# A layer of attention and feed-forward: the vector engine's turn in another order, the sums beside their compares, the window mask in the maximum

## Time and profile before

| | us |
|---|---|
| median of 3 runs (lowest, highest) | 1960.08 (1959.28, 1961.83) |
| the profiled execution | 1959.31 |
| its span, first to last instruction | 1957.5 |
| busy: PE, DVE, ACT, POOL | 1876.3, 1433.4, 1229.4, 1235.9 |
| stretch of the turns | about 22 to 1540 |
| a group of four turns in the loop | 46.8 |

### The profile page before, as it was taken

One profiled execution on the slowest core, in us unless ns is written; L12 is line 12 of the kernel. 1 busy time (PEld: TensorE's weight loads), 2 busy tenths in 40 slices (PEclk: granted clock), 3 DMA queues, 4 the chain that ended last, 5 costly groups with the idle time before them and its releaser, 6 DMA issues.

```text
span 1957.5 us, 42161 instructions
## 1 busy us (share of the span) xinstructions
PE 1876.3 (96%) x11698; PEld 1252.8 (64%) x11698; DVE 1433.4 (73%) x3926; ACT 1229.4 (63%) x4840; POOL 1235.9 (63%) x1150
## 2 busy tenths in 40 slices
PE   4999999999999999999999999999989979999997
PEld 3667677777777777776777676777666635444443
DVE  6998888888888888888888888888899644302022
ACT  5777777777777777777777777776666535312121
POOL 3777777777777777777777777777677521212121
PEclk8999999999999999999999999999999989999999
DMA  5000000000000000000000000000100042000000
GB/s 199 25 26 25 26 25 24 24 24 24 32 25 24 24 24 24 29 24 24 24 24 24 30 29 24 24 24 13 54 13 7 7 134 79 26 1 22 0 21 21
DMA packets 44353, 61.43 MB, mean 31 GB/s; under 512 B 4928, under 2 KB 18496, under 8 KB 44288
## 3 DMA queue, kind: packets, MB, share of 16 engines
q1 hardware_dynamic: 44288, 60.64, 9.6%
HBM read 47.97 MB, written 12.65 MB: 31 GB/s over the span
## 4 chain that ended last, share of the span: by engine, by line
PE 62%; DVE 16%; issue 14%; POOL 3%; ACT 2%; DVEq 1%; DMA 0%; SPq 0%; POOLq 0%; ACTq 0%
PE bank L1250 18%; PE bank L1239 8%; PE bank L1278 6%; PE bank L1221 4%; PE bank L1294 4%; PE bank L1315 4%; PE bank L1379 3%; PE bank L1287 3%; DVE f_s L963 2%; PE bank L1205 2%; PE bank L1304 2%; POOL hl L527 2%; DVE f_nrm L953 2%; PE bank L1270 1%; PE bank L1297 1%
## 5 line engine op out<-in xcount | busy, mean ns | idle before, releaser
L488 POOL TENSOR_TENSOR f_acc<-f_acc,f_s 128x512 f32<-128x512 f32 (+1 forms) x416 | 534.3, 1284 | 30.6 <-POOL f_acc L488 0.4
L1250 PE MATMUL bank<-wh,xh 128*128 (+2 forms) x1024 | 334.9, 327 | 7.3 <-DVE cumh L1099 6.2
L1250 PE MATMUL bank<-wl,xh 128*128 (+2 forms) x1024 | 335.0, 327 | 0.0
L1250 PE MATMUL bank<-wh,xl 128*128 (+2 forms) x1024 | 334.7, 327 | 0.0
L469 POOL TENSOR_TENSOR pr<-pr,rp 128x512 f32<-128x512 f32 x128 | 133.0, 1039 | 229.5 <-DVE rp L894 229.5
L963 DVE TENSOR_SCALAR f_s<-f_nrm 128x512 f32<-128x512 f32 (+1 forms) x480 | 240.9, 561 | 3.7
L575 ACT ACTIVATE qe<-bank,nqm 128x128 f32<-128x128 f32 x512 | 180.8, 365 | 80.3 <-DVE qs L823 57.2
L527 POOL TENSOR_TENSOR hl<-hf,hh 128x512 f16<-128x512 f32 (+1 forms) x44 | 50.8, 1155 | 283.7 <-ACT hh L754 283.7
L1379 PE MATMUL bank<-xh,w 128*128 (+3 forms) x704 | 224.8, 382 | 3.8 <-ACT sg L748 3.8
L603 ACT ACTIVATE pr<-bank,pmx 128x128 f32<-128x128 f32 x512 | 180.9, 367 | 37.5 <-DVE pmx L887 29.6
L1239 PE MATMUL bank<-wh,oT 128*128 (+1 forms) x512 | 194.0, 379 | 3.8 <-DVE xl L1019 1.4
(11 more groups left out here) (177 smaller groups left out, 4973.7 us busy)
## 6 DMA issues: line engine op xcount, KB each, us to landing
f_raw<-wf SPq DMA_DIRECT2D x30, 256.0 KB, 2.6
dequantised<-f_dq SPq DMA_DIRECT2D x30, 256.0 KB, 2.0
wt<-dequantised SPq DMA_DIRECT2D x30, 256.0 KB, 3.0
raw_qkv<-wq SPq DMA_DIRECT2D x29, 256.0 KB, 2.5
raw_o<-wo SPq DMA_DIRECT2D x29, 256.0 KB, 2.6
rows<-x SPq DMA_DIRECT2D x4, 1024.0 KB, 9.3
xr<-x SPq DMA_DIRECT2D x16, 256.0 KB, 3.6
out<-yo SPq DMA_DIRECT2D x16, 256.0 KB, 2.1
```

The lines of the kernel that those rows point to most:

```text
L488: nc.gpsimd.tensor_tensor(f_acc[:, 0:w], f_acc[:, 0:w], f_s[:, k % 8, 0:w], ALU.add)\
L1250: last = nc.tensor.matmul(dst, av, w[:, sl + c, lo:hi], start=(n == 0), stop=(n == 3 * NC - 1))
```

## The change

The mask's matmul (L1270) leaves PE. DVE's `p_max` becomes four instructions of 128x128, one for each head: each adds the mask `win` to the scores, negates the sum, writes it back into `SC` and reduces it to its minimum; one element is set to zero ahead of them. For tiles with p=0 the first two heads use `win0`, a copy of the right version of the mask that ACT makes in that turn. ACT's `p_exps` takes the scores with scale -1.

The scale `em` is now an exponential on ACT, whose bias `keep` is 0 or -1e30.

DVE's turn: `gla_k` and then, at p=0 instead of p=1, `nf4_end`; `add_out` moves ahead of `merge`; two compares stand between them (none at p=0), the rest after `state` and ahead of `p_max`. The compares are dealt out 4, 3, 4 and 4. The blocks of the next piece are taken at p=1 and `f_nrm` at p=3, both after the logs and ahead of `use_q`. `p_sums` moves behind `use_q`. POOL adds a compare in the turn in which it is made.

```diff
-NF4_STEPS = (range(0, 2), range(2, 6), range(6, 11), range(11, 15))
+NF4_STEPS = (range(0, 4), range(4, 7), range(7, 11), range(11, 15))
...
                 if l1.real():
                     softmax_q(l1)
-                    nf4_add(l1)
+                nf4_add(t)
+                if l1.real():
                     softmax_p(l1)
...
+            def head_mask(t):
+
+                if t.p == 0:
+                    nc.scalar.activation(win0[:], win[:, t.i % 2, 0:P], ACT.Copy).then_inc(s["head_mask"], 1)
...
                 nc.scalar.activation(edT[:, r, :], SM[:, P:P + 130], ACT.Exp)
+                if t.p == 0 and not (isinstance(t.i, int) and t.i == 0):
+                    nc.scalar.activation(em[:, 0, :], SM[:, 2 * P:2 * P + 1], ACT.Exp,
+                                         bias=keep[:].unsqueeze(2)[:, t.i % 2, :])
...
                     last = nc.scalar.activation(pr[:, r, j * P:(j + 1) * P], SC[:, j * P:(j + 1) * P], ACT.Exp,
-                                                bias=pmx[:, r, j:j + 1],
+                                                bias=pmx[:, r, j:j + 1], scale=-1.0,
...
                 k_exps(t)
+                head_mask(t)
...
             def p_max(t):
                 r = t.p % 2
                 wait_tile(dve, s["sc_done"], t)
-                nc.vector.tensor_reduce(pmx[:, r, :], SC[:].rearrange("p (h n) -> p h n", h=GRP), AX.X, ALU.max,
-                                        negate=True).then_inc(s["pmx_d"], 1)
+                nc.vector.memset(pause[:], 0.0)
+                for j in range(GRP):
+                    sl = slice(j * P, (j + 1) * P)
+                    mask = win[:, 1, sl] if t.p or j >= 2 else win0[:]
+                    last = nc.vector.tensor_tensor_reduce(SC[:, sl], SC[:, sl], mask, -1.0, -MASKED, ALU.add,
+                                                          ALU.min, pmx[:, r, j:j + 1])
+                last.then_inc(s["pmx_d"], 1)
...
                 if nxt.p == 0:
-                    nc.vector.tensor_tensor(em[:, 0, :], scale, keep[:, nxt.i % 2:nxt.i % 2 + 1] if isinstance(nxt.i, int)
-                                            else keep[:].unsqueeze(2)[:, nxt.i % 2, :], ALU.mult).then_inc(s["em_d"], 1)
-                    dve.wait_ge(s["em_d"], nxt.i)
                     scale = em[:, 0, :]
...
+            def nf4_normalise(i):
+                w = width_of(i)
+                dve.wait_ge(s["f_recd"], i + 1)
+                if not (isinstance(i, int) and i == 0):
+                    dve.wait_ge(s["f_sd"], i * 15)
+                nc.vector.tensor_tensor(blocks(f_nrm, w), blocks(f_raw, w),
...
             def turn(t):
                 use_k(t)
                 if l1.real():
                     q_sums(l1)
-                if t.p == 1 and not (isinstance(t.i, int) and t.i == 0):
+                    gla_k(l1)
+                if t.p == 0 and not first:
                     nf4_end(t.i - 1)
-                if l1.real():
-                    gla_k(l1)
+                if l3.real():
+                    add_out(l3)
...
+                split = 0 if t.p == 0 else 2
+                nf4(t, NF4_STEPS[t.p][:split])
                 if l2.real():
                     merge(l2)
-                if l3.real():
-                    add_out(l3)
-                if l2.real():
                     state(l2)
+                nf4(t, NF4_STEPS[t.p][split:])
                 if l1.real():
                     p_max(l1)
                 log_decay(t)
                 low_decay(t)
-                if t.p == 0:
-                    nf4_blocks(t.i)
-                else:
-                    nf4(t)
+                if t.p == 1 and not final:
+                    nf4_blocks(t.i + 1)
+                if t.p == 3 and not final:
+                    nf4_normalise(t.i + 1)
...
+                use_q(t)
                 if l1.real():
                     p_sums(l1)
-                use_q(t)
-                if l1.real():
                     gla_q(l1)
-                if t.p == 0:
-                    nf4(t)
...
             def scores(t):
-                nc.tensor.matmul(SC[:], identb[:], win[:, 1, :] if t.p else win[:, t.i % 2, :], start=True, stop=False)
+                if t.p == 0:
+                    pe.wait_ge(s["head_mask"], t.i + 1)
```

More of the change, by code:

```diff
@@ L214, in layer @@
         rp = sb("rp", [P, 2, GRP])
+        pause = sb("pause", [P, 1])
+        win0 = sb("win0", [P, P], BF16)
         f_max = sb("f_max", [P, 2, NF4_MAX // BLK])
@@ L245, in layer @@
             kmx_d nkm_a kabs_ev kneg_d krope_d g_d gl_d rks_d kt_d qmx_d nqm_a qrope_d rq_d qt_d pmx_d
-            rp_d pm_d pa_ev su_d em_d sr_d acc_d qrope_p krope_p qn_p pn_p
+            rp_d pm_d pa_ev su_d head_mask sr_d acc_d qrope_p krope_p qn_p pn_p
             wqk_sc wqk_hi wqk_lo wo_sc wo_hi wo_lo w0_hi raw_a raw_b consts z_id
@@ L520, in _ @@
             softmax_p(last_turn)
-            nf4_add(last_turn)
             def low_hidden(g, c):
@@ L937, in nf4_blocks @@
                 w = width_of(i)
+                if not (isinstance(i, int) and i < 2):
+                    dve.wait_ge(s["f_dqd"], i - 1)
+                if not (isinstance(i, int) and i == 0):
+                    dve.wait_ge(s["f_nrmd"], i)
                 dve.wait_ge(s["f_in"], i * 16 + 16)
@@ L947, in nf4_blocks, with nf4 @@
                 nc.vector.reciprocal(f_rec[:, 0:w // BLK], f_safe[:, 0:w // BLK]).then_inc(s["f_recd"], 1)
-            def nf4(t):
-                i, w = t.i, width_of(t.i)
-                if t.p == 0:
[L952 to L955, removed]
+            def nf4_normalise(i):
+                w = width_of(i)
+                dve.wait_ge(s["f_recd"], i + 1)
+                if not (isinstance(i, int) and i == 0):
+                    dve.wait_ge(s["f_sd"], i * 15)
+                nc.vector.tensor_tensor(blocks(f_nrm, w), blocks(f_raw, w),
+                                        f_rec[:, 0:w // BLK].unsqueeze(2).to_broadcast([P, w // BLK, BLK]), ALU.mult)\
+                    .then_inc(s["f_nrmd"], 1)
+            def nf4(t, steps):
+                i, w = t.i, width_of(t.i)
+                if t.p == 0 and len(steps):
                     dve.wait_ge(s["f_nrmd"], i + 1)
-                for k in NF4_STEPS[t.p]:
+                for k in steps:
                     if k >= 8:
@@ L1032, in turn @@
                 l1, l2, l3, n = t.back(1), t.back(2), t.back(3), number(t)
+                first, final = (isinstance(t.i, int) and t.i == i for i in (0, STEPS - 1))
                 use_k(t)
@@ L1035, in turn @@
                     q_sums(l1)
-                if t.p == 1 and not (isinstance(t.i, int) and t.i == 0):
+                    gla_k(l1)
+                if t.p == 0 and not first:
                     nf4_end(t.i - 1)
-                if l1.real():
-                    gla_k(l1)
+                if l3.real():
+                    add_out(l3)
+                if t.p == 0 and first:
+                    nf4_blocks(0)
+                    nf4_normalise(0)
+                split = 0 if t.p == 0 else 2
+                nf4(t, NF4_STEPS[t.p][:split])
                 if l2.real():
                     merge(l2)
-                if l3.real():
-                    add_out(l3)
-                if l2.real():
                     state(l2)
+                nf4(t, NF4_STEPS[t.p][split:])
                 if l1.real():
@@ L1279, in scores @@
                                                 qrT[:, r, b, 2 * hp:2 * hp + 2, :].rearrange("p h n -> p (h n)"), keys,
-                                                start=False, stop=(j == 3))
+                                                start=(j == 0), stop=(j == 3))
                 last.then_inc(s["sc_done"], 1)
@@ L1485, in constants @@
     cum /= 16.0
-    keep = np.ones((P, 2), np.float32)
-    keep[:, 0] = 0.0
+    keep = np.zeros((P, 2), np.float32)
+    keep[:, 0] = MASKED
     return {"cosc": cos, "sinc": sin, "winmask": win, "causal": cau, "cumsum": cum,
```

## The result

The kernel after takes 2024.79 us in the median of 4 runs (2023.71 to 2028.09), the kernel before in the runs beside them 1960.34 (1959.28 to 1961.83): a ratio of 1.033 with a 95% interval of 1.031 to 1.035. The forecast was 2037, with a range of its own from 2000 to 2080. The profiled execution is the longest of the four, 2028.09, with a span of 2026.0.

What follows compares the result with a forecast made beforehand. It took PE to bound the attention stage. Walking the engines' turns gave 2.75 us more per group: 66 over 24 steady groups plus 11 for eight end groups, 77 on 1959.3, so 2036, as a median 2037; range 2000 to 2080.

Steps and rivals of the forecast that it cites:

- p=3 late: In turn p=3 POOL's later chain makes the probabilities 0.7 late for PE; 0.68 us in the group's sum.
- p=0 late: In turn p=0 rotated q comes 1.2 us late and the merge costs another 0.15, together 1.36.
- p=1 late: In turn p=1 oT comes 1.0 us late, then the merge is late too: 1.56 in the group's sum.
- p=2 late: In turn p=2 the merge, behind compares held by POOL, comes late for PE: 0.83 us in the group's sum.
- The maximum: DVE's four masked reduces and a memset ahead of ACT's exponentials take 1.26 us instead of 0.6; bounds 0.9 and 2.3.
- f_nrm at p=3, rotated q at p=0: POOL's fourth add holds f_nrm, so use_q starts at 12.15 and rotated q comes 1.2 us late next turn.
- The merge at p=2, p=3 and p=1: DVE's compares, held by POOL's rotations and q product, delay the merge: done 6.3 at p=2 (wanted 5.9), 7.45 at p=1.
- oT at p=1: ACT's oT, behind the late maximum, is there 2.6 us into turn p=1 instead of 1.6: 1.0 late.
- The lock: A compare or two-SBUF-input DVE operation arriving while POOL works starts only about 0.13 us before POOL's instruction ends.
- second rival: POOL's softmax products don't lock DVE and the maximum is cheap (0.9): group 47.2 us, time 1970; chance 0.12.
- Rival 1: The turn is bound by PE, compares finding POOL at rest: group 45.1 to 46.2, time 1912 to some 1940; chance 0.24.
- Rival 3: The reduce on DVE is dear, the maximum taking 2.3 us: group 52.7, time 2110; chance 0.07.

Runs made afterwards that it cites:

- e9: The kernel after with f_nrm of p=3 moved from ahead of use_q to behind gla_q: 2000.87 us, 1.021 of the kernel before.
- e1: The kernel after with each of POOL's sums over 16 of its 512 columns, the rest left out: 1952.97 us, 0.997 of the kernel before.
- e6: The kernel before with f_nrm and the two compares of p=0 moved ahead of p_sums and use_q: 1985.86 us, ratio 1.013.
- e3: The kernel before with the mask in DVE's maximum and the scale em on ACT, in the old order: 1962.4 us, ratio 1.001.
- e4: The kernel after with no compare ahead of the merge, all between state and p_max: 2130.27 us, 1.087 of the kernel before.
- e2: The kernel after with the mask back on PE and one tensor_reduce as the maximum: 2014.72 us, 1.028 of the kernel before.
- e5: The kernel after with POOL adding each compare one turn later and nf4_end back at p=1: 2273.99 us, 1.162 of the kernel before.

## Why the prediction was right

Its mechanism held: the waits that it named came late in the turns that it named, and in each of the four turns by somewhat less than forecast. By its own steps, in us:

| step | predicted | measured |
|---|---|---|
| p=3 late | 0.68 | 0.52 |
| p=0 late | 1.36 | 1.30 |
| p=1 late | 1.56 | 1.28 |
| p=2 late | 0.83 | 0.62 |
| group over 46.80 | 2.75 | 2.05 |
| 24 steady groups | 66 | 50.9 |
| the eight end groups | 11 | 17 |
| maximum, all of it | 1.26 | 0.96 |

That the total came as near as it did is in part luck: the steady groups were put 15 too high and the end groups 6 too low. The span grew by 68.5 instead of 77. The upper end of the range doesn't follow from the working: even 22 more for the end groups gives 2059, and the rest up to 2080 has no term.

*The maximum* is the term that was mis-sized: 0.25 a reduce and not 0.29, and the memset lies under the first reduce (755.23 to 755.44 above), so 0.96 to 1.0. With 0.9 the walk had given 48.6 a group; the chip gave 48.85. I had chosen the value; the lower bound was nearly right, as the accumulator's read starts with the next reduce and costs nothing but the last one's. The Trainium skill ("VectorE: DVE Perf Modes", Two Vector instructions with no wait between them) says that an operation which writes out its accumulator is two instructions, and this trace agrees: they take 0.33 and 0.14. That they overlap, this trace adds.

*f_nrm at p=3, rotated q at p=0.* f_nrm meets POOL's last sum and takes 1.41; `use_q` starts 11.8 into the turn (12.15 predicted), and the transposes of rotated q 5.51 after p=0's start (5.6 predicted). e9 confirms the step by itself.

```profile
768.73 1.41 DVE L971 TENSOR_TENSOR f_nrm<-f_raw,f_rec 128x512 f32<-128x512 f32 x1
770.06 0.68 DVE L861 TENSOR_REDUCE qmx<-bank 128x4 f32<-128x512 f32 x1
```

*The merge at p=2, p=3 and p=1.* Late in all three, as forecast, by 0.6, 0.5 and (with ACT's part) 1.2. At p=2 and p=3 this has nothing to do with the sums: e1, with short ones, is as late there (0.6 and 0.5), and 0.5 late at p=1.

*oT at p=1* was sized too high: 0.44 late instead of 1.0, since the maximum was over 0.3 earlier against the turn. The view of waits names the copy of `ktT` there, the instruction before oT in ACT's list, so the chain is the one foretold but not the wait. `kt` ended 4.9 into the turn (787.58 - 782.66; 5.1 predicted).

*The lock* works in the turns as the walk had it, and *POOL's softmax products hold DVE too*, the open point of the second rival: in the turn p=2 above the second compare is over only 0.28 after the q product, and in e6 f_dq takes 1.47 beside it. By the Trainium skill ("SBUF — State Buffer", Who interferes with whom) a DVE instruction with two SBUF inputs contends with any GpSimd instruction that reads SBUF, and f_dq's 1.47 instead of 0.66 agrees. This rival is out, though the cheap maximum that it assumed was true.

*Rival 1* failed where it was said to: the lateness of the four turns is 3.72, not under 1.7. *Rival 3* is excluded by the reduce's 0.33.

*The end groups* lost 17 and not 11: the first four 3.1 each, more than a steady one, the last three 1.4 each. Taking them at half was a guess. *The FFN stage* is unchanged to about 1 us.

What I did not foretell well is e3: for the mask alone I expected most of its gain from the same rows, forgetting that the turn with a late `kt` isn't PE's to shorten.

## What to carry to other kernels

Two engines that lock each other out make every instruction's place in one list a matter of the other list: before a move, write down what the other engine runs at the new place, and what stands behind the moved instruction. "Behind the instruction that PE waits for" is not enough as a rule: f_dq moved there met POOL at rest and gave 19 us, but all the compares moved there (e4) met POOL's sums and cost 105 us more than the kernel after. f_dq moved by three lines was worth no less (19 us) than the mask's move with its companions (16 us), a matmul taken off the engine that is 96% busy; and that matmul gave nothing in e3, where `kt` was late.

## What the runs showed of the hardware

- With POOL at work a compare of 0.42 took up to 1.50, f_dq and f_nrm of 0.66 to 0.69 took, in the mean of a kernel, 1.38 (f_nrm before) to 1.78 (f_nrm in e2). POOL loses too, but less: its sums were 1.28 in the mean before and 1.36 after.
- A POOL product with an operand of 128x4 spread over 512 columns (L464; L462 in e6) holds DVE as one with two full operands does: in e6 f_dq, begun 0.11 behind it, took 1.47 and ended 0.54 after it.
- Four reduces with an accumulator, of 128x128 from PSUM with a bf16 operand from SBUF: 0.33 each, one per 0.25, the accumulator's read 0.14 beside the next. They were not held by POOL: 316 to 322 ns in the mean in every kernel that has them, and at 755.23 in the kernel after they run under a sum.
- With PE idle for 2.0 us ahead of a turn and 3.6 us in it, the turn's mean granted clock was 0.81 (e5); with stands of 0.6 (after) and of 1.4 (e5, the two turns behind) it stayed at 1.00.
